# Recurrent mixture-of-experts layer: lists of a step worked chunk by chunk, outputs two chunks behind the gates, start constants formed later

## The reference

```python
def step(carry, xt):
    h, c = carry
    gates = xt @ Wi + h @ Wh + b                      # 128 -> 4*128
    i_, f_, g_, o_ = jnp.split(gates, 4, axis=-1)
    c = sigmoid(f_) * c + sigmoid(i_) * tanh(g_)
    h = sigmoid(o_) * tanh(c)
    return ((h, c), h @ Wo + bo)
...
logits = flat_x @ router_w + router_b
top_vals, top_idx = top_k(logits, 2)                  # of 8 experts
rw = softmax(top_vals, axis=1)
expert_x = mask * flat_x                              # zero where not routed
y = einsum('ken,nk,keno->no', mask, rw, out)
```

## Time and profile before

| | us |
|---|---|
| median of 3 runs (2971.86 to 2985.92) | 2976.36 |
| the profiled execution's own time | 2996.18 |
| its span, first to last instruction | 2994.2 |
| PE busy in the span | 2452.0 (82%) |
| DVE, ACT, POOL busy | 1559.4, 1334.8, 381.1 |

### The profile page before, as it was taken

How to read it: one execution, slowest core, us unless ns; L and a number is a source line. 1 busy time by engine, 2 the same in 40 slices (tenths; PEclk the granted TensorE clock), 3 DMA queues, 4 the chain that set the end, 5 groups by cost and what they waited for, 6 DMA issues and landing times. The chain is left out here.

```text
span 2994.2 us, 53498 instructions
## 1 busy us (share of the span) xinstructions
PE 2452.0 (82%) x17887; PEld 1819.6 (61%) x17887; DVE 1559.4 (52%) x3485; ACT 1334.8 (45%) x3207; POOL 381.1 (13%) x577
## 2 busy tenths in 40 slices
PE   7389999977999969799877777784699999973895
PEld 4155555545988947456757676773466666643783
DVE  3288888854256055315533444433676776742124
ACT  2277777742144125455314445443355555531341
POOL 0000000000710710000072020201100000003344
PEclk8589999987999979899759999997799999985996
DMA  3366666633246113010127676773423322202571
GB/s 115 121 183 192 193 193 190 192 115 127 75 149 199 43 44 133 22 37 1 45 87 235 190 221 199 223 224 104 100 65 76 81 63 70 57 3 73 188 229 57
DMA packets 245793, 367.88 MB, mean 123 GB/s; under 512 B 48090, under 2 KB 182738, under 8 KB 244834
## 3 DMA queue, kind: packets, MB, share of 16 engines
q1 hardware_dynamic: 228162, 335.17, 37.1%
q0 software_dynamic: 9216, 18.89, 2.1%
q10 hardware_dynamic: 8224, 11.36, 1.3%
HBM read 219.82 MB, written 108.31 MB: 110 GB/s over the span
## 5 line engine op out<-in xcount | busy, mean ns | idle before, releaser
L3501 ACT ACTIVATE lstm_gate<-lstm_g_ps,lstm_bv 128x128 f32<-128x128 f32 x741 | 212.2, 371 | 300.5 <-PE lstm_g_ps L3431 176.3
L3428 PE MATMUL lstm_g_ps<-lstm_xT,lstm_w 128*128 128x128 f32 x1482 | 271.0, 291 | 38.8 <-issue 31.9
L4165 DVE TENSOR_REDUCE caus_nmx<-caus_a_ps 128x4 f32<-128x512 f32 (+5 forms) x352 | 215.7, 641 | 107.7 <-PE caus_a_ps L3976 104.9
L4113 ACT ACTIVATE caus_probsT<-caus_s_ps 128x512 f32<-128x512 f32 (+4 forms) x352 | 189.8, 559 | 150.5 <-PE caus_s_ps L3995 147.0
L3428 PEld LDWEIGHTS lstm_g_ps<-lstm_xT,lstm_w 128*128 128x128 f32 x1482 | 219.2, 202 | 53.5 <-issue 52.2
L3976 PE MATMUL caus_a_ps<-caus_ks,caus_qs 96*128 96x128 f32 (+6 forms) x768 | 180.4, 327 | 10.6 <-DVE caus_nmx L4165 10.5
L3995 PE MATMUL caus_s_ps<-caus_qs,caus_ks 98*128 98x128 f32 (+6 forms) x768 | 186.3, 333 | 0.5 <-ACT caus_probsT L4113 0.4
L1081 DVE TENSOR_REDUCE rel_nmax<-rel_s_ps 128x1 f32<-128x746 f32 x192 | 178.8, 931 | 7.8 <-PE rel_s_ps L919 0.8
L934 PE MATMUL rel_t_ps<-tower_ident,rel_probs 128*128 128x128 f32 x1152 | 169.7, 285 | 11.3 <-DVE rel_probs L1061 7.7
L3431 PE MATMUL lstm_g_ps<-lstm_state,lstm_w 128*128 128x128 f32 x912 | 176.3, 275 | 0.0
L1037 ACT ACTIVATE rel_probs<-rel_s_ps,rel_nmax 128x746 f32<-128x746 f32 x192 | 172.2, 897 | 2.3 <-DVE rel_nmax L1081 2.2
(11 more groups left out here) (506 smaller groups left out, 5202.7 us busy)
## 6 DMA issues: line engine op xcount, KB each, us to landing
lstm_w<-in_lstm_w SPq DMA_DIRECT2D x114, 512.0 KB
moe_w<-in_moe_w SPq DMA_DIRECT2D x38, 578.0 KB
moe_ew<-in_moe_w SPq DMA_DIRECT2D x33, 578.0 KB
lstm_w<-in_lstm_w SPq DMA_DIRECT2D x57, 256.0 KB
lstm_xs<-attn_zeros SPq DMA_DIRECT2D x20, 608.0 KB, 7.6
caus_qs<-caus_xh SPq DMA_DIRECT2D x128, 93.2 KB, 2.2
caus_ks<-caus_xh SPq DMA_DIRECT2D x120, 93.2 KB, 2.2
lstm_x<-lstm_xs SPq DMA_DIRECT2D x40, 256.0 KB
```

Source lines behind the costliest of these rows:

```text
L3428: mm = nc.tensor.matmul(bank[:, at_q], wm[:, WI_AT[q] * P:(WI_AT[q] + 1) * P], xT[n % 3][:, i * P:(i + 1) * P], start=True, stop=(f == t))
L3501: nc.scalar.activation(gate[q % 3][:, v, i * P:(i + 1) * P], g_ps[m % 4][:, v * P:(v + 1) * P], ACT.Tanh if v == 2 else ACT.Sigmoid, bias= ...
L4113: nc.scalar.activation(probsT[j][0:rows, heads[0]:heads[-1] + 1, q0 - j * P:q1 - j * P], heads_of(s_ps[at % 3][0:rows, :], heads, q1 - q0) ...
L4165: nc.vector.tensor_reduce(nmx[0:rows, slot, heads[0]:heads[-1] + 1, t:t + 1], heads_of(bank[0:rows, :], heads, k1 - k0), AX.X, ALU.max, ne ...
```

## The change

1. **Order.** Within a step the chunks go by block position, and within a position by list: (j=0: f=0..t), (j=4: f=0..t), ...
2. **Outputs two chunks behind.** During chunk n PE emits, behind each block's gates, an output matmul of chunk n-2 (before: of the block four earlier). DVE's `copy_out` in chunk n is that of chunk n-2 (before: n-1).
3. **Counts ahead of the constants.** `start_gates(1)` moves behind the count matmuls. `start_gates(2)` and `(3)` move into the loop, behind the second block of chunks 1 and 4, with their sums, squashings, cells and states spread over DVE's and ACT's groups; they use a bank of the input-transpose ring. PE no longer waits for them before the loop.
4. **`block_values`** 1, 2, 3 move to groups 1, 11 and 13.

SP's program is not edited. The core of the diff:

```diff
     for t in range(STEPS):
-        for f in range(t + 1):
-            for j in range(0, R_BLOCKS, R_CHUNK):
+        for j in range(0, R_BLOCKS, R_CHUNK):
+            for f in range(t + 1):
...
+        start_at = {1: 2, 4: 3}
         for n in range(N):
             USES.append(("x", n, 0))
+            if n - 2 in start_at:
+                USES.append(("b", start_at[n - 2], 0))
...
             def start_gates(s):
                 pe.wait_ge(st_ready, s)
-                pe.wait_ge(z_ready, s)
+                if s >= 2:
+                    pe.wait_ge(tr_free, use_at["b", s, 0] - 1)
...
-            start_gates(1)
             pe.wait_ge(marked, 1)
             nc.tensor.matmul(counts, lower[:, 0, :], marks[:], start=True, stop=False)
...
-            start_gates(2)
+            start_gates(1)
             pe.wait_ge(gh_ready, 1)
...
-            start_gates(3)
...
-            pe.wait_ge(z_ready, S)
+            pe.wait_ge(z_ready, 2)
...
-            for m in range(M + R_CHUNK):
-                if m < M:
-                    n, t, f, j, i = BLOCKS[m]
-                    c = f * R_BLOCKS + j
-                    expert[m] = pe.value_load(table[0:1, c:c + 1], min_val=0, max_val=E - 1)
-                    gates(m)
+            for n in range(N + 2):
+                t, f, j0, width, m0 = CHUNKS_R[min(n, N - 1)]
+                earlier = list(range(CHUNKS_R[n - 2][4], CHUNKS_R[n - 2][4] + CHUNKS_R[n - 2][3])) if n >= 2 else []
+                for i in range(width if n < N else 0):
+                    c = f * R_BLOCKS + j0 + i
+                    expert[m0 + i] = pe.value_load(table[0:1, c:c + 1], min_val=0, max_val=E - 1)
+                    gates(m0 + i)
                     if i == 0 and n + 2 < N:
                         turn(n + 2)
+                    if i == 1 and n in start_at:
+                        start_gates(start_at[n])
...
-                if m >= R_CHUNK:
-                    output(m - R_CHUNK, expert.pop(m - R_CHUNK))
+                    if earlier:
+                        output(earlier[0], expert.pop(earlier.pop(0)))
+                while earlier:
+                    output(earlier[0], expert.pop(earlier.pop(0)))
...
-            start_sums(1)
-            start_cells(1)
             dve.wait_ge(ranked, 1)
...
-                if q == 1:
-                    for f in range(1, S):
-                        block_values(f)
                 if q >= 1:
                     states(q - 1)
                 if q % 2 == 1:
-                    if n >= 1:
-                        copy_out(n - 1)
+                    if n >= 2:
+                        copy_out(n - 2)
...
+                if q == 3 or q == 9:
+                    start_sums(2 if q == 3 else 3)
+                elif q == 5:
+                    start_cells(2)
+                elif q == 7:
+                    start_states(2)
+                elif q in (1, 11, 13):
+                    block_values({1: 1, 11: 2, 13: 3}[q])
             states(len(GROUPS_R) - 1)
+            copy_out(N - 2)
             copy_out(N - 1)
```

More of the change, by code:

```diff
@@ L3228, in recurrent_experts @@
         counts = o_ps[0][:, 0:S * (R_TILES + 1) * E].rearrange("p (s j e) -> p s j e", s=S, e=E)
-        b_ps = o_ps[1][:, 0:4 * E].rearrange("p (g e) -> p g e", e=E)
         bias_ge = bias[:].rearrange("p e g -> p g e")
@@ L3253, in recurrent_experts, with start_ps, sums_ready @@
         use_at = {use: u for u, use in enumerate(USES)}
+        def start_ps(s):
+            bank = o_ps[1] if s == 1 else tr[use_at["b", s, 0] % 2]
+            return bank[:, 0:4 * E].rearrange("p (g e) -> p g e", e=E)
+        def sums_ready(eng, s):
+            if s < 2:
+                eng.wait_ge(z_ready, s + 1)
+            else:
+                eng.wait_ge(tr_free, use_at["b", s, 0] + 1)
         def rows(dram, n):
@@ L3352, in start_gates @@
                 pe.wait_ge(st_ready, s)
-                pe.wait_ge(z_ready, s)
+                if s >= 2:
+                    pe.wait_ge(tr_free, use_at["b", s, 0] - 1)
                 for e in range(E):
                     for q in range(4):
-                        mm = nc.tensor.matmul(b_ps[:, q, e:e + 1], wh[:, e, q * P:(q + 1) * P], H[:, s - 1, e:e + 1],
+                        mm = nc.tensor.matmul(start_ps(s)[:, q, e:e + 1], wh[:, e, q * P:(q + 1) * P], H[:, s - 1, e:e + 1],
                                               start=True, stop=True)
-                mm.then_inc(b_full, 1)
+                mm.then_inc(b_full if s == 1 else tr_full, 1)
             def turn_z(n):
@@ L3467, in _, with squash_gates @@
         def _(act):
-            def squash_start(s):
-                act.wait_ge(z_ready, s + 1)
+            def squash_gates(s):
+                sums_ready(act, s)
                 if s > 0:
@@ L3474, in squash_start, with squash_cell @@
                 nc.scalar.activation(sg[:, 3, :], value[:, s, 3, :], ACT.Sigmoid).then_inc(squashed, 1)
+            def squash_cell(s):
                 act.wait_ge(cell_ready, s + 1)
                 nc.scalar.activation(sg[:, 4, :], value[:, s + 1, 8, :], ACT.Tanh).then_inc(squashed, 1)
-            squash_start(0)
+            squash_gates(0)
+            squash_cell(0)
             for n in range(TOK_TILES // 4):
@@ L3488, in _ @@
                 nc.scalar.copy(gT[:, n * BANK:(n + 1) * BANK], g_ps[n % 2][0:2 * E, :]).then_inc(gT_ready, 1)
+            squash_gates(1)
+            squash_cell(1)
             def gates(q):
@@ L3516, in _ @@
                     squash(q - 1)
+                if q == 4:
+                    squash_gates(2)
+                if q == 6:
+                    squash_cell(2)
         @block.vector
@@ L3524, in start_sums @@
                 if s > 0:
-                    dve.wait_ge(b_full, s)
-                    nc.vector.tensor_tensor(value[:, s, 0:4, :], b_ps, value[:, 0, 0:4, :], ALU.add).then_inc(z_ready, 1)
+                    if s == 1:
+                        dve.wait_ge(b_full, 1)
+                    else:
+                        dve.wait_ge(tr_full, use_at["b", s, 0] + 1)
+                    nc.vector.tensor_tensor(value[:, s, 0:4, :], start_ps(s), value[:, 0, 0:4, :], ALU.add).then_inc(
+                        z_ready if s == 1 else tr_free, 1)
                 else:
@@ L3544, in block_values @@
                 if f > 0:
-                    dve.wait_ge(z_ready, f + 1)
+                    sums_ready(dve, f)
                     dve.wait_ge(cell_ready, f)
@@ L3610, in _ @@
             places(0)
-            start_states(1)
             c.link(nc.vector.scalar_tensor_tensor(out=ends[:], in0=taken[:], scalar=float(P), in1=base[:], op0=ALU.mult, op1=ALU.add))
@@ L3621, in _ @@
             places(1)
-            block_values(0)
-            start_sums(2)
             dve.wait_ge(exp_ready, 1)
@@ L3630, in _ @@
                                     ALU.mult).then_inc(gh_ready, 1)
-            start_cells(2)
+            block_values(0)
             places(2)
-            start_states(2)
             places(3)
+            start_sums(1)
             for n, (b, half) in enumerate(CHUNKS):
@@ L3638, in _ @@
                 nc.vector.tensor_tensor(h, h, g_ps[2 + n % 2][:, 0:HALF], ALU.add).then_inc(bo_added, 1)
-            start_sums(3)
+            start_cells(1)
+            start_states(1)
             def copy_rows(n):
```

2 lines of the change are left out of this document (removed).

## The result

The changed kernel takes 2886.46 us (median of 3 runs, 2879.12 to 2888.57) against 2976.36: ratio 0.9687, interval 0.9641 to 0.9733, 90 us less. Its profiled execution took 2888.57 us. The forecast was 2884.

The account below looks back on a forecast made before the run. DMA transfers, 329 us, were taken as the floor of steps 1 to 3. 21 us sooner there plus 72.5 saved minus 1 at the end made 92.5, from the median 2884; range 2850 to 2910, chance 0.54.

Parts of the forecast that it names:

- Before the loop: Start of the stage: the loop begins at 1513 instead of 1544.3, 31 us sooner, bounds 27 to 35.
- Step 0: First step of the loop: 55 us against 45.1, with two start_gates at 13.8 us each; bounds 45 to 62.
- What goes in steps 1 to 3: PE's waits at output matmuls for states, 56.7 us, and the 30.5 us of issue go, with the slow matmuls.
- Steps 1 to 3 as a sum: Transfers 329, late weights 48, mixed rows 15, block_values 6: 398 us against 470.6, 72.5 saved.
- The floor is the transfers' 329 us: Steps 1 to 3: DMA share 0.70 of 470.6 us makes 329 at full share, more than PE's 313.
- The late weights: Steps 1 to 3: PE waits 3.0 us for weights after f == t chunks in 15 rounds; 48 us in all.
- The clock: Rival, steps 1 to 3: the clock drops at each round, 2.1 us per restart, 32 us, so 2916; chance 0.07.
- The new order smooths little; it sets what follows what: Steps 1 to 3: the chunk order leaves the mean load unchanged, since PE's and the transfers' floors shrink alike; no size given.
- Absorbed late weights: Rival, steps 1 to 3: SP's wait never reaches PE, the 48 us go, 2836; chance 0.15.
- Transfers cannot go faster: Rival, steps 1 to 3: transfers stay at 248 GB/s, the part takes 437 us, so 2923; chance 0.16.
- Slower: Rival, steps 1 to 3: SP's in-order queue makes every chunk late, at 5 us each 3061; chance 0.04.
- no change: Rival, steps 1 to 3: the state's wait only moves, to ACT's banks or SP, at 3.1 us per chunk; chance 0.04.

Follow-up runs that it names:

- deep_inputs_back_late: deep_inputs with PE's transposes of the mixed rows moved behind the chunk's last block; 2814.52 us, ratio 0.9422 to before.
- deep_inputs: The changed kernel with eight weight buffers instead of four from block 20 on and inputs loaded five chunks ahead instead of four; 2834.88 us, ratio 0.9488 to before.
- store_later: The changed kernel with SP storing chunk n-3 instead of n-2 behind chunk n; 2882.54 us, ratio 0.9666 to before.

## Why the prediction was right, point by point

**Before the loop: right.** 31 us were forecast. The kernels with the old start give 78.5 against 45.3: 33. The counts, the covering `start_gates(1)` and the gate weights came in the predicted order. That the two numbers are so near is in part luck: the loop was to begin about 1513 and began at 1502.9, since `start_gates(1)` took 9.8 us where 13.8 were put, and the way from the gate weights to the loop 16.7 where 23.5 were; the latter held the pauses that only the profiled execution of before shows, and they made the start of before as much later.

**Step 0: right, a term too large.** Forecast 55 us, measured 51.1. The stall of the earlier trace rows is gone, and the two `start_gates` cost 11.7 + 10.0 instead of 27.6: each began at a granted clock of 1.00 and ended at 0.50 (0.59 and 0.70 over the whole), where the 13.8 of the earlier trace rows ran at 0.50 throughout.

**What goes in steps 1 to 3: right.** The waits for states and the "issue" fell from 87.2 to 2.8 us, and the lag alone took 86 us from the part (469.1 to 383.2).

**Steps 1 to 3 as a sum: right in size, wrong in its terms.** Forecast 329 + 48 + 15 + 6 = 398, measured 406 (411 by the window of the earlier trace rows's kind).
- *"The floor is the transfers' 329 us"* is the step that failed. `deep_inputs_back_late` loads the same bytes and does the part in 334 us with 9.5 us of clock loss and 12.9 of waits; its DMA share of 0.88 makes 293 us. The 329 came from a share of busy time, and that share is no constant of the work: the same transfers made 0.78 x 406.3 = 317 us in after and 293 there. PE's 313 is the nearer floor: 313 + 41 of weights + 15.5 of mixed rows + 1.8 + 1.0 + 29.6 of clock is 402 of the 406, though waits at a low clock are counted twice in it.
- *The late weights* were 48 forecast, 41.0 measured: ten waits of 2.2 to 4.2 us behind chunks f == t make 33 of it, where 15 of 3.0 were predicted. Four short ones in or behind such chunks make 2.2. The other ten, 5.6 us with one of 1.71, stand behind blocks of lists f < t, which the prediction had named as a sign of being wrong. The place is right in the main, and the causal story is one of three: SP's wait for the copy, the landing under load and the short lead of four buffers together.
- *The clock* was left to a rival at 0.07, and the text said that below 0.95 the forecast would be wrong. It was 0.93. The rival held in part: 29.6 us against 13.8 before, so 16 of the 32 that it priced. In the sum, which has no clock term, 29.6 us are missing; the floor's excess of 16, the 7 too many for weights and the 6 for `block_values`, against 2.8 of waits left, nearly make up for them. That the sum came out is luck.
- *"The new order smooths little; it sets what follows what"* was half a step: the second half is where its cost lies. It puts a short chunk in front of a long one's 2.1 MB in every round, where a lead counted in blocks is shortest in time; some 33 us by the ratios, found only by putting the old order back.

**The rivals.** *Absorbed late weights*: no, 41 us. *Transfers cannot go faster*: no; after moved 239 GB/s, the last kernel 293. *Slower* and *no change*: an f < t chunk did cover most of the way to the copy, as argued, though 5.6 us of waits stand behind such blocks.

The Trainium skill (TensorE: Matmul & The Clock Gate, HAM oscillation) describes a loop whose bursts of matmuls are shorter than its waits for data, and in which every burst starts throttled. Here the bursts are longer than the waits, and not every one starts so: the granted clock was 0.50 behind a wait of 4.19 us and 1.00 behind one of 2.96 us; the rows stand in the last section.

## What to carry to other kernels

Count a prefetch's lead in time over the shortest work that can lie in it, not in buffers: four buffers gave 4.0 us over the chunks of one kind of list and (78 - 2 - 16) x 0.112 = 6.7 over those of the other, and eight removed 41 us of waits without a byte less. When several causes end at one due time, taking one away moves little; add lead, which covers them all, before hunting for the one to blame. Try each part of a change alone and left out: here the part that the prediction gave no term cost 1.1% where the rest gave 4.2%.

## What the hardware showed unexpectedly

Waits of a few microseconds did not all cost clock. Windows of after behind a wait of 2.96 us (it ended at 1737.61) and behind one of 4.19 us (at 1819.60); the third last column is the granted clock:

```profile
1738.00:1742.00 4.00, 4.00 (x38) 4.00 (x38) 0.69 (x1) 1.14 (x4) 0.00 (x0) 1.00 0.97 294
...
1819.60:1825.00 5.40, 5.40 (x25) 5.40 (x26) 0.69 (x1) 1.14 (x4) 4.31 (x8) 0.50 0.98 326
```

After the first PE goes on at 2.4 GHz, after the second at 1.2 GHz. The mixed rows' waits were dearer than their length: in `deep_inputs` two of them (5.08 us to 1597.47 and 3.78 us to 1602.34) go with 8 us at 0.50, from 1598.1 to 1606.1.

A busy PE is not always at full clock. The window of `start_gates(3)` in before, of which PE was busy 100%:

```profile
1530.20:1544.00 13.80, 13.80 (x65) 13.72 (x64) 0.54 (x1) 0.00 (x0) 11.30 (x18) 0.50 0.13 44
```

In after PE was as busy through `start_gates(2)` (1512.24 to 1523.90), and the clock fell from 2.4 to 1.2 GHz in its course:

```profile
1512.30:1514.30 2.00, 2.00 (x21) 2.00 (x20) 1.97 (x2) 1.19 (x4) 1.79 (x2) 1.00 0.82 233
...
1515.00:1523.70 8.70, 8.70 (x42) 8.70 (x43) 0.93 (x3) 0.00 (x0) 7.10 (x12) 0.50 0.20 65
```

And a load's landing is no constant: 512 KB took 4.6 us in the median in after and 5.4 in `store_later`, where SP issues them without the wait for a copy ahead.
